# New slots for the side work between the drive matmuls of a fused tokenizer, scan and FFN kernel

## The chip, the cores and the metric

One core of a Trainium2 chip. The metric is the device time of one execution in microseconds (us), the median of several runs. "Granted clock" is the share of TensorE's full clock (2.4 GHz) that the chip let through; it has two levels here, 2.4 and 1.2 GHz.

## What is computed

For 32 images of 3x224x224 the reference cuts 196 patches of 16x16x3, normalises them, multiplies by a 768x256 matrix and normalises again (tokens). 77 text tokens of 256 values are put behind them, so that there are 273 positions. Then a gated scan and a gated FFN are added, each on a layer-normalised input:

```python
x_sub = x[:, ::2]                               # every second position
x_proj, gate = split(rmsnorm(x_sub) @ w_in.T + b_in)
h = tanh(h * A + xt[:, :, None] * Bm)           # one step per sub-sampled position
y = h @ Cm.sum(0) + Dv * xt
out = repeat((y * silu(gate)) @ w_out.T + b_out, 2)
h = h + out
h = h + (silu(n(h) @ wg.T) * (n(h) @ wu.T)) @ wd.T
```

The scan's state has 256 x 64 values for each of 32 batch rows, and its steps depend on each other.

## The kernel before, in words

The 273 positions go through the kernel in 20 groups of 14 (14 image groups, 6 text groups, the last one shorter). In the body of group i five stages run side by side on five different groups: the raw pixels of group i+1 are normalised ("ahead"), group i becomes tokens, a projection and a gate ("pre"), group i-1 is scanned ("scan"), group i-2 gets its attention output, residual and the first half of the FFN ("post"), and group i-3 the down projection ("down").

The scan sets the order of everything. A group has 7 steps of 8 chunks, 56 **slots**. A slot is one `grow` on VectorE (line 771: state times A into a PSUM bank, four banks in turn), one `drive` on TensorE (1218: adds x times B) and one `squash` on ScalarE (976: tanh). `grow(n)` waits for `squash(n-4)`, so VectorE can be four slots ahead at most. After the drive of every eighth slot (3, 11, 19, ...) TensorE also runs `read_step` (1228), which sums y. The `read_step` of slot 3 closes the group before.

All other work ("side work") is put behind the grow, drive or squash of a slot that a table names: `PLANS` (lines 65 to 113) gives for each kind of group the slot of each piece, for each engine. Kinds are "first" (group 0, no scan, slots mean order only), "second", "image" (bodies 2 to 13, of which 3 to 12 are a loop), "text" (14 to 19), "last" and "tail". GpSimd has no slots, only an order (`POOL_ORDER`, lines 116 to 139). Each engine runs its list strictly in order and waits on semaphores, so a piece whose input is late holds the slots behind it.

Pieces that matter here, with their lines:

- `shrink` (1389 to 1403), 8 pieces of 6 matmuls, the down projection; the first waits for `act_low_part` 5 on GpSimd (1158).
- `turn` (1250) and `xT_copy` (990), 8 each: transposes of pixels on TensorE and their copies on ScalarE; `embed` (1277), 12 pieces of 4 recorded matmuls.
- The **y chain**: `read_step` at slot 3, `y_copy` on ScalarE (978), four DMAs to memory (651), two back (657), `gating` on GpSimd (1116, two instructions at 1121 and 1125), and `attend(0)` and `attend(1)` on TensorE (1326, matmuls at 1335 and 1338), which wait for it.
- The **raw load**: three DMAs of 448 KB (352). The sync queue issues them only when all 7 `normalise` pieces of ScalarE (984) and of GpSimd (1136) are done with the pixels before; in its program they stand ahead of the gate load (644) and of the y chain's DMAs. `raw_patch` (776, instruction 778), 14 pieces on VectorE, wait for them.
- `residual`, `res_stats`, `res_variance`, `res_shift` (VectorE, 860 to 886), `fx_apply` and `fxT_copy` (ScalarE), `turn_fx` (TensorE), then `ffn` gate and up pieces (1361), `ffn_silu`, `ffn_product`, `act_high_part`, `act_low_part`.
- In group 0 `ffn_max`, `bias_split` and `flag_large` (VectorE, 498, 420, 539) and `count_large` make a flag that TensorE reads before its first drive (1526).

## Time and profile before

| | |
|---|---|
| median of 3 runs | 1426.93 us (1425.58 to 1428.28) |
| the profiled execution | 1428.12 us |
| its span, first to last instruction | 1426.3 us |
| TensorE matmul busy | 1224.9 us (86% of the span) |
| VectorE, ScalarE, GpSimd busy | 1085.5, 1001.3, 434.4 us |
| mean granted clock | 0.943 |
| a loop image group (ten) | 72.27 to 74.53 us |
| a text group | 51.78 us and up |

Times in the rows are microseconds from the span's start. PE is TensorE, PEld its weight loads, DVE VectorE, ACT ScalarE, POOL GpSimd, SPq the sync queue. The first 84.49 us are set-up and group 0, and 67.20 us follow the start of the last drive.

### The profile page before, as it was taken

The page shows a single profiled execution, that of the slowest core. Times are in us where ns is not written, and L with a number is a line of the kernel's source. Part 1 is how long each engine was busy: PE and PEld are TensorE (multiplying, and loading weights), DVE is VectorE, ACT ScalarE, POOL GpSimd, SP SyncE. Part 2 cuts the span into 40 slices and gives each one's busy share as a digit, 9 for nine tenths or more (in the row PEclk, how much of TensorE's full clock was granted, in tenths as well). Part 3 has the DMA queues.
Part 4 walks back from the last instruction along what each step waited for, and adds up shares of the span by engine and source line. Part 5 has one row for each costly group of instructions (what it writes and reads, how often), then busy time and mean ns, then how long its engine had stood idle before and what let it go on. Part 6 is the DMA issues. An engine that isn't in the chain of part 4 may idle for free.

```text
span 1426.3 us, 25870 instructions
## 1 busy us (share of the span) xinstructions
PE 1224.9 (86%) x7137; PEld 662.5 (46%) x7137; DVE 1085.5 (76%) x2412; ACT 1001.3 (70%) x1955; POOL 434.4 (30%) x437
## 2 busy tenths in 40 slices
...
GB/s 183 56 75 28 104 31 112 28 115 26 116 26 115 17 123 6 132 6 126 16 120 22 116 26 104 38 81 23 92 67 94 78 77 76 80 77 58 75 36 15
DMA packets 154671, 99.60 MB, mean 70 GB/s; under 512 B 129057, under 2 KB 143265, under 8 KB 153281
## 3 DMA queue, kind: packets, MB, share of 16 engines
...
## 4 chain that ended last, share of the span: by engine, by line
PE 36%; issue 22%; DMA 10%; ACT 9%; POOL 9%; DVE 8%; SPq 5%; POOLq 0%; DVEq 0%; ACTq 0%
PE Y L1228 6%; PE U L1218 6%; DMA y_scr<-y_fx 6%; PE P L1385 5%; PE P L1288 5%; PE P L1386 5%; DVE U L771 3%; PE P L1321 3%; DMA yT<-y_scr 3%; ACT h L976 3%; ACT rawn L987 2%; SPq L651 2%; DVE act L891 1%; POOL yT L1121 1%; POOL zT L1125 1%
## 5 line engine op out<-in xcount | busy, mean ns | idle before, releaser
L771 DVE TENSOR_TENSOR U<-h,a_col 128x512 f32<-128x512 f32 x1096 | 704.5, 689 | 147.7 <-ACT h L976 146.7
L976 ACT ACTIVATE h<-U 128x512 f32<-128x512 f32 x1096 | 608.1, 603 | 240.8 <-PE U L1218 239.1
L1218 PE MATMUL U<-x_diag,b_st 128*128 128x512 f16 x1096 | 370.2, 388 | 63.0 <-DVE U L771 45.1
L1228 PE MATMUL Y<-h,read_st 128*32 128x512 f32 x2192 | 271.0, 613 | 0.7 <-ACT h L976 0.7
L1218 PEld LDWEIGHTS U<-x_diag,b_st 128*128 128x128 f16 x1096 | 105.1, 100 | 220.8 <-DVE U L771 146.0
L1160 POOL TENSOR_TENSOR xT_act<-act,xT_act 128x448 f16<-128x448 f32 x114 | 117.5, 1040 | 195.1 <-ACT xT_act L1060 194.1
L1288 PE MATMUL P<-tok_w,xT_act 128*112 128x256 f32 x672 | 169.7, 391 | 2.3 <-ACT xT_act L993 2.3
L1288 PEld LDWEIGHTS P<-tok_w,xT_act 128*112 128x112 f32 x672 | 120.2, 182 | 54.0 <-issue 21.2
L1400 PE MATMUL P<-down_w,xT_act 128*112 128x256 bf16 x480 | 118.5, 282 | 6.9 <-POOL xT_act L1160 4.6
L1228 PEld LDWEIGHTS Y<-h,read_st 128*32 128x32 f32 x2192 | 58.2, 111 | 138.4 <-issue 114.9
L1401 PE MATMUL P<-down_w,xT_act 128*112 128x256 bf16 x480 | 117.4, 279 | 0.0
L891 DVE SCALAR_TENSOR_TENSOR act<-fsg,P 128x448 f32<-128x448 f32 x118 | 72.6, 615 | 52.5 <-PE P L1386 51.9
L1121 POOL TENSOR_TENSOR yT<-yT,gate_in 128x448 f32<-128x448 f32 x20 | 22.7, 1134 | 260.9 <-DMA yT<-y_scr 260.9
L993 ACT ACTIVATE xT_act<-P 128x384 f32<-128x384 f32 x112 | 83.2, 804 | 15.1 <-PE P L1273 13.2
L1385 PE MATMUL P<-fx_split,gate_w 128*128 128x448 f16 x228 | 81.7, 358 | 10.8 <-DVE fx_split L896 10.1
L1385 PE MATMUL P<-fx_split,up_w 128*128 128x448 f16 x236 | 86.4, 366 | 4.6 <-DVE act L891 4.6
L778 DVE BATCH_NORM_STATS2 raw_st<-raw 96x6 f32<-96x256 f32 x196 | 70.1, 410 | 24.8 <-DMA raw<-in_x 24.8
L1386 PE MATMUL P<-fx_split,up_w 128*128 128x448 f16 x236 | 86.3, 366 | 0.0
L1056 ACT ACTIVATE fsg<-P 128x448 f32<-128x448 f32 x114 | 62.4, 547 | 33.2 <-PE P L1386 30.4
L1386 PE MATMUL P<-fx_split,gate_w 128*128 128x448 f16 x228 | 81.8, 359 | 0.0
L1321 PE MATMUL P<-xaT,in_w 128*128 128x224 f32 x320 | 76.0, 369 | 6.0 <-ACT xf L1026 4.9
L1110 POOL TENSOR_TENSOR res_s<-res_s,half_th 112x4 f32<-112x4 f32 x20 | 20.6, 1028 | 189.8 <-DVE res_s L881 189.8
...
## 6 DMA issues: line engine op xcount, KB each, us to landing
...
```

What stands on the lines that cost most here:

```text
L771: dve.tensor_tensor(U[bank_of(slot)][:, :].rearrange("p (l b) -> p l b", b=B), h[:, (slot - CHUNKS) % RING, :].rearrange("p (l b) -> p l b ...
L891: dve.scalar_tensor_tensor(act[:, k, :], fsg[:, k % 2, :], ACT_SCALE * DEQUANT, up_bank(k, scan)[:, 0:4 * PT], ALU.mult, ALU.mult).then_in ...
L976: sc.activation(h[:, slot % RING, :], U[bank_of(slot)][:, :], ACT.Tanh, scale=1.0 / U_SCALE).then_inc(squashed, 1)
L1160: gp.tensor_tensor(act_lo[:, k, :], act[:, k, :], act_hi[:, k, :], ALU.subtract).then_inc(act_lo_done, 1)
L1218: pe.matmul(U[bank_of(slot)][:, :], b_st[:, c, :], x_diag[:, c, :, t * B:t * B + B], start=False, stop=True, skip_group_check=True).then_i ...
L1228: mm = pe.matmul(Y[c4 * 32:c4 * 32 + 32, :], read_st[:, t, half, :], h[:, (t * CHUNKS + half * RG + c4) % RING, :], start=(t == 0 and half ...
L1288: mm = pe.matmul(P[1 - k // 2][0:PT, (k % 2) * D:(k % 2) * D + D], xT[:, f, k // 2, (k % 2) * PT:(k % 2) * PT + PT], tok_w[:, f, :], start ...
L1321: mm = pe.matmul(P[1][:, k * TOK:k * TOK + TOK], in_w[:, j, e0:e0 + 128], xaT[:, j, :], start=(j == 0), stop=(j == DB - 1))
L1385: pe.matmul(bank, half, fx_hi[:, j, :], start=(j == 0), stop=False)
L1386: mm = pe.matmul(bank, half, fx_lo[:, j, :], start=False, stop=(j == DB - 1))
L1400: pe.matmul(bank, act_hi[:, f, k * PT:k * PT + PT], half, start=(f == 0), stop=False)
L1401: mm = pe.matmul(bank, act_lo[:, f, k * PT:k * PT + PT], half, start=False, stop=(f == HB - 1))
```

## The change

Only the tables `PLANS` and `POOL_ORDER` change. No instruction, wait, transfer or buffer is added or removed. For the image kind: `y_copy` goes from slot 0 to 3; `shrink` pieces 2 to 7 go ahead of where they were (five of the eight now stand ahead of slot 3's `read_step`, which had two); `turn` starts one slot later and ends at slot 16, where both `attend` pieces now stand; ScalarE's seven `normalise` pieces go from slots 47 to 55 to slots 43 to 53, and GpSimd's end ahead of `act_low_part` 4 and 5; the 14 `raw_patch` pieces go from 3 at slot 11, 8 at 15 and one each at 16, 17 and 18 to 2 at 12, 4 at 14, 1 at 15, 4 at 16 and 3 at 17. In "text" the residual's pieces are spread, in "first" the flag's pieces are mixed with others. The plans "second" and "tail" and GpSimd's other orders are changed in the same manner.

```diff
--- before.py
+++ after.py
@@ -64,76 +64,75 @@
 
 PLANS = {
     "image": dict(
-        shrink=(1, 1, 3, 3, 4, 4, 6, 7), turn=(7, 7, 8, 10, 12, 12, 12, 14), attend=(15, 16), average=(19, 21),
-        embed=(17, 19, 19, 20, 20, 21, 24, 25, 25, 27, 28, 28), turn_fx=(32, 32), ffn_gate=(34, 37, 40, 42, 45, 49),
-        ffn_up=(34, 39, 42, 43, 50, 52), turn_xa=(35,), project=(40, 40, 46, 48), finish=(6, 9), raw_patch=(11, 11,
-        11, 15, 15, 15, 15, 15, 15, 15, 15, 16, 17, 18), raw_means=(21,), raw_deviation=(23,), raw_variance=(24,),
-        res_stats=(21,), res_variance=(21,), res_shift=(25,), fx_low_part=(34, 34), tok_stats=(28, 32),
-        tok_shift=(29, 40), ln_stats=(35,), ln_shift=(35,), raw_shift=(32,), x_low_part=(43,), ffn_product=(36, 40,
-        44, 47, 51, 55), y_copy=(0,), xT_copy=(7, 7, 11, 11, 12, 12, 12, 14), fx_apply=(25, 26, 27, 28),
-        fxT_copy=(31, 31), tok_normalise=(27, 39), ln_apply=(34,), xaT_copy=(35,), x_copy=(39,), gate_silu=(47,),
-        ffn_silu=(32, 36, 39, 42, 45, 50), act_high_part=(41, 42, 43, 48, 49, 53), normalise=(47, 51, 54, 55, 55,
-        55, 55), residual=(21,)),
+        shrink=(1, 1, 1, 2, 2, 5, 6, 6), turn=(8, 8, 10, 12, 12, 13, 14, 16), attend=(16, 16), average=(19, 21),
+        embed=(17, 18, 19, 19, 21, 22, 23, 25, 27, 28, 28, 28), turn_fx=(30, 32), ffn_gate=(34, 38, 39, 41, 44, 49),
+        ffn_up=(34, 38, 42, 43, 50, 52), turn_xa=(37,), project=(40, 40, 46, 47), finish=(8, 9), raw_patch=(12, 12,
+        14, 14, 14, 14, 15, 16, 16, 16, 16, 17, 17, 17), raw_means=(19,), raw_deviation=(22,), raw_variance=(23,),
+        res_stats=(20,), res_variance=(20,), res_shift=(25,), fx_low_part=(34, 34), tok_stats=(27, 32),
+        tok_shift=(30, 37), ln_stats=(35,), ln_shift=(36,), raw_shift=(39,), x_low_part=(44,), ffn_product=(37, 40,
+        46, 47, 52, 55), y_copy=(3,), xT_copy=(7, 9, 9, 12, 12, 12, 12, 14), fx_apply=(25, 25, 27, 27),
+        fxT_copy=(30, 30), tok_normalise=(28, 37), ln_apply=(34,), xaT_copy=(36,), x_copy=(40,), gate_silu=(47,),
+        ffn_silu=(32, 37, 39, 42, 46, 50), act_high_part=(42, 42, 43, 44, 52, 53), normalise=(43, 44, 50, 50, 51,
+        53, 53), residual=(19,)),
     "text": dict(
-        shrink=(6, 7, 8, 9, 13, 16, 17, 18), attend=(23, 24), turn_fx=(34, 34), ffn_gate=(36, 39, 41, 46, 49, 50),
-        ffn_up=(37, 39, 45, 48, 49, 52), turn_xa=(26,), project=(29, 30, 31, 33), finish=(11, 21), res_stats=(31,),
-        res_variance=(31,), res_shift=(32,), fx_low_part=(36, 36), ln_stats=(23,), ln_shift=(24,), x_low_part=(45,),
-        ffn_product=(39, 45, 48, 50, 51, 55), y_copy=(3,), fx_apply=(31, 31, 31, 31), fxT_copy=(32, 32),
-        ln_apply=(23,), xaT_copy=(27,), x_copy=(30,), gate_silu=(31,), ffn_silu=(36, 39, 41, 46, 49, 50),
-        act_high_part=(45, 50, 51, 54, 55, 55), residual=(31,)),
+        shrink=(3, 5, 7, 7, 10, 15, 15, 17), attend=(21, 24), turn_fx=(34, 34), ffn_gate=(35, 38, 41, 45, 49, 52),
+        ffn_up=(36, 39, 44, 48, 50, 53), turn_xa=(27,), project=(29, 29, 32, 32), finish=(13, 20), res_stats=(32,),
+        res_variance=(32,), res_shift=(34,), fx_low_part=(36, 36), ln_stats=(22,), ln_shift=(28,), x_low_part=(46,),
+        ffn_product=(39, 43, 47, 51, 54, 55), y_copy=(2,), fx_apply=(31, 31, 31, 31), fxT_copy=(32, 32),
+        ln_apply=(26,), xaT_copy=(27,), x_copy=(29,), gate_silu=(31,), ffn_silu=(35, 38, 41, 47, 50, 53),
+        act_high_part=(43, 44, 48, 48, 53, 53), residual=(29,)),
     "last": dict(
-        shrink=(4, 7, 8, 9, 10, 13, 15, 16), attend=(23, 25), turn_fx=(33, 37), ffn_gate=(42, 45, 49, 51, 53, 55),
-        ffn_up=(42, 47, 51, 53, 55, 55), finish=(13, 19), res_stats=(37,), res_variance=(40,), res_shift=(46,),
-        fx_low_part=(48, 51), ffn_product=(52, 52, 53, 53, 53, 53), y_copy=(4,), fx_apply=(33, 38, 40, 42),
-        fxT_copy=(45, 49), ffn_silu=(53, 54, 54, 54, 55, 55), act_high_part=(54, 54, 55, 55, 55, 55),
-        residual=(30,), y_next=(50,)),
+        shrink=(2, 4, 5, 5, 7, 10, 14, 14), attend=(22, 26), turn_fx=(33, 33), ffn_gate=(35, 38, 45, 51, 51, 55),
+        ffn_up=(37, 42, 49, 53, 55, 55), finish=(15, 19), res_stats=(35,), res_variance=(40,), res_shift=(49,),
+        fx_low_part=(49, 55), ffn_product=(55, 55, 55, 55, 55, 55), y_copy=(7,), fx_apply=(35, 41, 41, 45),
+        fxT_copy=(45, 47), ffn_silu=(51, 54, 55, 55, 55, 55), act_high_part=(54, 54, 55, 55, 55, 55),
+        residual=(33,), y_next=(47,)),
     "first": dict(
-        turn=(0, 0, 0, 0, 0, 0, 0, 0), average=(27, 30), embed=(12, 13, 14, 16, 16, 16, 20, 20, 21, 22, 25, 27),
-        turn_xa=(27,), project=(30, 38, 52, 52), raw_patch=(7, 8, 11, 11, 11, 12, 12, 12, 12, 13, 13, 16, 24, 32),
-        raw_means=(35,), raw_deviation=(38,), raw_variance=(39,), tok_stats=(12, 27), tok_shift=(14, 32),
-        ln_stats=(31,), ln_shift=(34,), raw_shift=(44,), x_low_part=(48,), xT_copy=(1, 1, 2, 2, 3, 4, 6, 6),
-        tok_normalise=(21, 47), ln_apply=(22,), xaT_copy=(22,), x_copy=(30,), gate_silu=(55,), normalise=(50, 54,
-        54, 55, 55, 55, 55), count_large=(55,), flag_large=(55,), weight_copy=(2, 7, 7, 18, 20), clear_banks=(22,),
-        sum_c=(29,), read_scale=(42,), bias_split=(53,), ffn_cast=(4, 16, 25, 32, 42), ffn_max=(51, 53, 53, 53, 53,
-        53)),
+        turn=(0, 0, 0, 0, 0, 0, 0, 0), average=(13, 23), embed=(3, 4, 4, 4, 4, 4, 4, 4, 4, 4, 4, 8), turn_xa=(16,),
+        project=(19, 19, 29, 34), raw_patch=(1, 1, 1, 1, 1, 1, 1, 1, 1, 4, 9, 10, 15, 21), raw_means=(31,),
+        raw_deviation=(35,), raw_variance=(49,), tok_stats=(7, 24), tok_shift=(11, 35), ln_stats=(27,),
+        ln_shift=(27,), raw_shift=(52,), x_low_part=(51,), xT_copy=(1, 1, 1, 2, 2, 2, 4, 4), tok_normalise=(5, 33),
+        ln_apply=(20,), xaT_copy=(28,), x_copy=(34,), gate_silu=(55,), normalise=(42, 43, 43, 44, 44, 44, 44),
+        count_large=(52,), flag_large=(55,), weight_copy=(0, 3, 5, 5, 10), clear_banks=(17,), sum_c=(13,),
+        read_scale=(46,), bias_split=(45,), ffn_cast=(0, 11, 17, 39, 52), ffn_max=(38, 52, 53, 53, 54, 55)),
     "second": dict(
...
     "tail": dict(
...
 }
 
 
 POOL_ORDER = {
     "image": (
         ("gating", 0), ("res_rsqrt", 0), ("raw_rsqrt", 0), ("token_rsqrt", 0), ("token_tiles", 0), ("ln_rsqrt", 0),
-        ("normalise", 0), ("normalise", 1), ("normalise", 2), ("token_rsqrt", 1), ("token_tiles", 1),
-        ("act_low_part", 0), ("act_low_part", 1), ("normalise", 3), ("act_low_part", 2), ("act_low_part", 3),
-        ("act_low_part", 4), ("normalise", 4), ("skip_term", 0), ("act_low_part", 5), ("normalise", 5),
-        ("normalise", 6)),
+        ("token_rsqrt", 1), ("token_tiles", 1), ("normalise", 0), ("act_low_part", 0), ("normalise", 1),
+        ("act_low_part", 1), ("act_low_part", 2), ("normalise", 2), ("skip_term", 0), ("normalise", 3),
+        ("act_low_part", 3), ("normalise", 4), ("normalise", 5), ("normalise", 6), ("act_low_part", 4),
+        ("act_low_part", 5)),
     "text": (
-        ("gating", 0), ("ln_rsqrt", 0), ("res_rsqrt", 0), ("act_low_part", 0), ("skip_term", 0),
-        ("act_low_part", 1), ("act_low_part", 2), ("act_low_part", 3), ("act_low_part", 4), ("act_low_part", 5)),
+        ("gating", 0), ("ln_rsqrt", 0), ("res_rsqrt", 0), ("act_low_part", 0), ("act_low_part", 1),
+        ("skip_term", 0), ("act_low_part", 2), ("act_low_part", 3), ("act_low_part", 4), ("act_low_part", 5)),
...
```

## Rows read from the trace of the kernel before

**Rows 1.** Busy time of each engine by stretch: loop groups of 56 slots, all ten summed.

```profile
core 0: us, PE busy (x) PEld busy (x) DVE busy (x) ACT busy (x) POOL busy (x), PEclk, DMA share, GB/s
...
363.28:435.55 72.27, 63.94 (x381) 35.71 (x381) 57.59 (x135) 53.42 (x105) 24.67 (x26) 0.98 0.28 70
...
654.14:728.67 74.53, 66.52 (x381) 36.82 (x382) 57.57 (x135) 53.30 (x105) 24.65 (x26) 0.93 0.28 68
...
sum 732.43, PE 650.09 PEld 360.87 DVE 575.95 ACT 533.91 POOL 246.58; mean PE 65.01 PEld 36.09 DVE 57.60 ACT 53.39 POOL 24.66
```

**Rows 2.** Groups by shape, whole run: busy, mean ns, idle before, releaser.

```profile
L771 DVE TENSOR_TENSOR U<-h,a_col 128x512 f32<-128x512 f32 x1096 | 704.5, 689 | 147.7 <-ACT h L976 146.7
...
L1400 PE MATMUL P<-down_w,xT_act 128*112 128x256 bf16 x480 | 118.5, 282 | 6.9 <-POOL xT_act L1160 4.6 <-DVE xT_act L906 2.3
...
L778 DVE BATCH_NORM_STATS2 raw_st<-raw 96x6 f32<-96x256 f32 x196 | 70.1, 410 | 24.8 <-DMA raw<-in_x 24.8
```

**Rows 3.** Waits, whole run: total us, times, longest us.

```profile
PE P L1335 <- POOL zT L1125: 30.1, 10, 3.1
...
DVE raw_st L778 <- DMA raw<-in_x: 24.8, 12, 10.9
```

**Rows 4.** Timeline of TensorE, loop group from 363.28: attend(0).

```profile
384.14 0.54 PE L1335 MATMUL P<-bias_row,bias_one 96*112 96x512 bf16 x1 [2.92 <-POOL zT L1125]
384.47 1.91 PE L1338 MATMUL P<-out_w,zT 128*112 128x256 f32 x4
```

**Rows 5.** Timeline of the sync queue, the same group.

```profile
367.00 1.36 SPq L352 DMA_DIRECT2D raw<-in_x  x3
...
369.45 2.56 SPq L651 DMA_DIRECT2D y_scr<-y_fx  x4
378.14 1.26 SPq L657 DMA_DIRECT2D yT<-y_scr  x2
```

**Rows 6.** Timeline of ScalarE, the same group.

```profile
364.60 2.08 ACT L987 ACTIVATE rawn<-raw,raw_s 96x256 f32<-96x256 f32 x4
...
368.44 0.60 ACT L982 ACTIVATE y_fx<-Y 128x512 f32<-128x512 f32 x1 [1.28 <-PE Y L1228]
```

**Rows 7.** Busy time: slots 12 to 20 of that group, of the last image group; slots 31 to 35.

```profile
377.91:393.42 15.51, 11.88 (x66) 7.22 (x63) 11.94 (x39) 7.39 (x14) 2.27 (x2) 0.89 0.34 87
963.79:974.73 10.94, 10.06 (x63) 6.04 (x60) 7.65 (x18) 7.26 (x14) 0.27 (x2) 1.00 0.24 61
405.93:412.35 6.42, 3.98 (x22) 1.78 (x20) 6.02 (x18) 4.47 (x10) 0.29 (x1) 1.00 0.00 0
```

**Rows 8.** Timeline of the sync queue, group from 148.39.

```profile
149.72 1.26 SPq L352 DMA_DIRECT2D raw<-in_x  x3
...
153.81 1.96 SPq L651 DMA_DIRECT2D y_scr<-y_fx  x4
160.61 1.24 SPq L657 DMA_DIRECT2D yT<-y_scr  x2
```

**Rows 9.** Timeline of the sync queue, text group from 1122.07.

```profile
1127.09 1.85 SPq L651 DMA_DIRECT2D y_scr<-y_fx  x4
1130.41 1.28 SPq L657 DMA_DIRECT2D yT<-y_scr  x2
```

**Rows 10.** Busy time: last image group, and a text group.

```profile
949.15:1018.32 69.17, 63.54 (x378) 34.64 (x378) 51.45 (x102) 53.39 (x104) 20.33 (x21) 0.98 0.21 56
...
1070.29:1122.07 51.78, 48.50 (x301) 23.49 (x301) 45.36 (x85) 42.50 (x86) 11.78 (x12) 1.00 0.30 82
```

**Rows 11.** Timeline of VectorE ahead of the first drive.

```profile
65.70 2.87 DVE L501 TENSOR_REDUCE large<-act 128x1 f32<-128x1536 f32 x2
...
71.18 0.46 DVE L422 CAST bias_row<-rows 1x256 bf16<-1x256 f32 x1
...
74.86 0.15 DVE L541 TENSOR_SCALAR large_flag<-Y 1x1 int32<-1x1 f32 x1
```

**Rows 12.** Timeline of TensorE: the first drive.

```profile
84.49 0.58 PE L1218 MATMUL U<-x_diag,b_st 128*128 128x512 f16 x1 [12.99 <-issue]
```

More of the change, by code:

```diff
@@ L99 @@
-    "second": dict(
-        turn=(0, 0, 0, 0, 0, 1, 2, 2), average=(21, 22), embed=(2, 2, 6, 7, 9, 13, 23, 23, 25, 25, 28, 31),
-        turn_xa=(34,), project=(36, 39, 47, 47), raw_patch=(5, 5, 6, 6, 6, 7, 11, 14, 14, 14, 17, 17, 19, 19),
-        raw_means=(21,), raw_deviation=(22,), raw_variance=(23,), tok_stats=(25, 36), tok_shift=(26, 40),
-        ln_stats=(31,), ln_shift=(32,), raw_shift=(28,), x_low_part=(47,), xT_copy=(0, 0, 0, 0, 0, 0, 0, 1),
-        tok_normalise=(24, 39), ln_apply=(31,), xaT_copy=(35,), x_copy=(43,), gate_silu=(51,), normalise=(35, 48,
-        53, 54, 54, 55, 55), ffn_turn=(37, 40, 41, 43, 46, 49, 51, 54, 55, 55, 55), ffn_even=(37, 42, 46, 51, 53,
-        55), ffn_odd=(42, 46, 54, 55, 55)),
@@ L107 @@
-    "tail": dict(
-        shrink=(0, 0, 0, 0, 0, 5, 6, 6), attend=(2, 2), turn_fx=(7, 12), ffn_gate=(18, 43, 43, 44, 49, 53),
-        ffn_up=(42, 48, 51, 52, 54, 54), finish=(0, 2), res_stats=(0,), res_variance=(0,), res_shift=(22,),
-        fx_low_part=(29, 36), ffn_product=(41, 42, 53, 54, 55, 55), fx_apply=(0, 0, 0, 0), fxT_copy=(5, 12),
-        ffn_silu=(15, 17, 18, 22, 29, 42), act_high_part=(21, 21, 32, 53, 53, 53), residual=(0,), act_low_tail=(49,
-        54, 54, 55, 55, 55)),
+        shrink=(1, 1, 1, 2, 2, 5, 6, 6), turn=(8, 8, 10, 12, 12, 13, 14, 16), attend=(16, 16), average=(19, 21),
@@ new lines @@
+    "second": dict(
+        turn=(2, 2, 2, 2, 2, 2, 3, 3), average=(20, 21), embed=(3, 3, 5, 7, 7, 14, 23, 25, 26, 26, 29, 32),
+        turn_xa=(35,), project=(36, 37, 41, 47), raw_patch=(4, 4, 4, 4, 5, 6, 8, 13, 14, 14, 15, 15, 21, 21),
+        raw_means=(21,), raw_deviation=(22,), raw_variance=(23,), tok_stats=(23, 39), tok_shift=(26, 43),
+        ln_stats=(30,), ln_shift=(34,), raw_shift=(30,), x_low_part=(47,), xT_copy=(1, 2, 2, 2, 2, 2, 2, 3),
+        tok_normalise=(26, 40), ln_apply=(35,), xaT_copy=(35,), x_copy=(39,), gate_silu=(50,), normalise=(28, 30,
+        35, 41, 46, 47, 49), ffn_turn=(39, 39, 40, 43, 43, 46, 52, 54, 55, 55, 55), ffn_even=(39, 41, 44, 51, 54,
+        54), ffn_odd=(43, 47, 54, 55, 55)),
@@ L113 @@
+    "tail": dict(
+        shrink=(1, 1, 1, 1, 1, 5, 5, 7), attend=(1, 3), turn_fx=(28, 29), ffn_gate=(43, 45, 47, 53, 53, 53),
+        ffn_up=(45, 50, 52, 52, 54, 55), finish=(0, 5), res_stats=(0,), res_variance=(0,), res_shift=(3,),
+        fx_low_part=(12, 19), ffn_product=(41, 47, 48, 49, 52, 52), fx_apply=(0, 0, 0, 0), fxT_copy=(0, 1),
+        ffn_silu=(16, 18, 22, 30, 45, 45), act_high_part=(17, 20, 39, 40, 51, 55), residual=(0,), act_low_tail=(45,
+        47, 50, 50, 55, 55)),
 }
```

16 lines of the change are left out of this document (8 added, 8 removed).

## The prediction

> **What bounds the kernel now.** I read the busy time by stretch first. In a loop group TensorE is busy 64 to 66.5 us of 72.27 to 74.53, more than VectorE (57.6) and ScalarE (53.4); the ten take 732.43, 73.24 each [rows 1]. With the same matmuls the best such a group can reach is the 63.94 us busy of the quietest one, less what half clock added to it; the rest is waits and half clock. So I looked for the wait that holds TensorE longest. It is `attend(0)`: ten waits for `gating`, 30.1 us in all [rows 3]. In the timeline it stands idle 2.92 us, and the four matmuls behind it then run at 1.2 GHz (1.91 us) [rows 4].
>
> Why is the y chain late? The sync queue of the group, which starts at 363.28, shows it. The raw load is issued at 367.00, 3.7 us into the group; the y store at 369.45 to 372.0; the load back, which waits for the store to land, only at 378.14 [rows 5], and `attend` starts 6.0 us after that [rows 4]. From the first y store to the load back are 8.7 us. In a text group, which has no raw load, they are 3.3 us [rows 9]; in the group from 148.39, where the raw load was issued 1.3 us into the group, 6.8 us, and the load back stands at 12.2 instead of 14.9 [rows 8]. The y store lands when the 1.3 MB of pixels ahead of it have drained. The raw load itself waits for four `normalise` of ScalarE that end at 366.68, behind slot 55 [rows 6].
>
> A control stands in the same trace: the last image group has the same plan, but no raw load and no `raw_patch`. Its slots 12 to 20 take 10.94 us at granted clock 1.00, against 15.51 at 0.89 in a loop group [rows 7]. The 4.57 us are the stall, its half clock and patches on VectorE together. The whole group takes 69.17 [rows 10], 4.1 less than the mean loop group.
>
> **The change, part by part** (against the profiled execution's 1428.12 us, which is 1.19 over the median of the runs; its span is 1426.3).
>
> *Raw load and y chain, image groups.* `normalise` moves so that one squash and two `normalise` less stand behind slot 53's pieces; at 0.5 us a piece (four in 2.08, [rows 6]) ScalarE ends them 2.0 to 2.5 us earlier, and the raw load goes out at 1.2 to 1.7 into the group. GpSimd's, which now stand ahead of `act_low_part` 4 and 5, need only `raw_shift` (slot 39) and end before that; the gate's store to memory, for which the sync queue waits ahead of the raw load, needs `skip_term`, which GpSimd now runs before them too. Five shrinks instead of two stand ahead of slot 3's `read_step`; a piece of 3 and 3 matmuls takes about 0.74 us (118.5 / 480 x 3, [rows 2]), so `y_copy`, now from 368.44 (5.2 into the group, [rows 6]), ends 2.2 us later, about 8.0. By the text group's pace the load back could then go at 8.0 + 3.3 + 0.3 = 11.6, by the drained queue (12.2, 1.32 after group start, [rows 8]) at 12.2 to 12.5. The later one decides, 12.4, so `attend` may start at 18.4 instead of 20.9. The plan brings TensorE there at 17.6 + 0.22 (slot 16) + 0.4 (`turn(7)`), 18.2 at the earliest. Stall left: 0 to 0.3 us.
>
> *The patches.* Cover is what they lose. Before, 11 of 14 ran at slots 15 to 18, under the stall. Now two stand at 12, four at 14, one at 15, seven at 16 and 17: 14 x 0.41 = 5.7 us [rows 2]. From slot 12 to 16 VectorE has five grows at 0.64 us (704.5 / 1096, [rows 2]) and seven patches, 6.1 us. Against them stand some 3.1 us of TensorE (four drives, four turns and their waits for `xT_copy`, my estimate from the 10.94 us of the control) and a lead that VectorE can have, two slots, 1.3 us, so 1.7 would be bare. At 16 and 17 seven patches and two grows, 4.2 us, lie beside slot 16's turn, both attends (2.1 us: attend(0) alone took 2.3 at 1.2 GHz [rows 4], so about 1.1 each at 2.4), two drives and an embed, 4 us: nothing more is bare than what the first part leaves. I take 1.6; bounds 0 and 5.7. Net for slots 12 to 20: -4.57 + 1.6, -3.0 us a group.
>
> *Start and end of a group.* `shrink(0)` still waits for `act_low_part(5)`, which has no earlier input; the eight shrinks now fill the time in which `y_copy` no longer blocks ScalarE from slot 0. -0.2 us. ScalarE carries 1.5 us more of `normalise` before slot 53, but its lag behind the drives is what it was, since all seven stood before the next group's squashes already: 0, with +0.7 as the bound if that cover is gone.
>
> *Slots 30 to 35.* `turn_fx(0)` moves to slot 30, but needs the first two adds of `tok_stats(1)`, on VectorE at 32, as before; `raw_shift` (1.2 us) no longer stands ahead of them. -0.4 us. TensorE is busy 3.98 of 6.42 us there [rows 7]; the mean group's 73.24 is above the quiet one's 72.27 by drops that come after such stretches and the first stall. Nothing fills it in the new plan. I keep the drops: +0.8 a group over the quiet one.
>
> A loop group: 72.27 - 3.0 - 0.2 - 0.4 + 0.8 = 69.5, say 69.6: 3.6 below 73.24, -36 for ten. Bounds: 68.3 (the control without its one drop, -49) and 72.3 (-9).
>
> *Group 0.* The flag is set at 74.86, after `ffn_max` from 65.70 and `bias_split` from 71.18 [rows 11]; the first drive follows at 84.49 [rows 12]. `bias_split` (3.7 us) and `ffn_max(0)` (1.7) go into earlier idle time, but `raw_variance` now stands behind them, and with it `x_low_part` slips 1.6 us and `raw_shift` behind GpSimd's power. Net -2.2, bounds -4.3 and +2.
>
> *The other groups.* The two early scans -1. Text: residual's shift moves behind two more grows, `turn_fx` starts 0.8 us later, an earlier `x_copy` gives back 0.3: +0.5 for each of six, +3; bounds -3 and +9, since a longer wait can cost clock. The last plan puts `ffn_gate(4)` ahead of `ffn_up(3)` on one bank and `y_next` ahead of `fxT_copy(1)`: +1.5, bounds -2 and +4.
>
> Sum: -36 - 2.2 - 1 + 3 + 1.5 = -34.7. 1428.1 - 34.7 = 1393.4; less 1.2 for the median, 1392.
>
> **The price of half clock.** From 0.98 to 0.93 of granted clock a loop group goes from 72.27 to 74.53 us [rows 1]: 7 us more at 1.2 GHz cost 2.3, a third, because TensorE is not the bound in all of them. The Trainium skill (TensorE: Matmul & The Clock Gate, Terms) prices it at the throttled time times one half; by that the drops that go would bring some 6 us more than I take.
>
> **Rivals.** (1) *The clock can't be laid out.* Of two groups of the same plan one ran at 0.98 (363.28) and one at 0.93 (654.14) [rows 1], so where a drop falls is not the plan's alone. If the stall goes but as much half clock stays, 1.5 us a group are not won: +15, 1407. The Trainium skill (TensorE: Matmul & The Clock Gate, What's actually happening) has the hardware's activity monitor run free of the kernel's start, which would speak for this; no run here shows it yet. Against: the control group has no drop in slots 12 to 20.
> (2) *VectorE takes over.* The patches lie bare for 3 us rather than 1.6, ScalarE is late at slots 43 to 55 by 0.7: +2.1 a group, 1413. For: VectorE has 57.6 us of work, in lumps.
> (3) *Slower.* In slots 12 to 18 every patch lies bare, 5.7 us against the 4.57 won: +1.1 a group, +11, and with text, last group and group 0 as above, 1440. It turns when 11 of the 14 patches are bare. Against: both attends stand over seven of them.
> (4) *No effect*, the raw load goes out no earlier, because `act_high_part(5)` ahead of the last `normalise` waits for VectorE's slot 55: -9 to 0, 1424.
>
> **How the numbers follow.** Forecast (1378 to 1402) 0.55, rival 1 0.15, rival 2 0.14, rival 3 0.09, rival 4 0.07. About 2.9 us (0.2%) is what a measurement can tell from no change. Rival 4 gives half to "same". Faster 0.87, same 0.04, slower 0.09. The range runs from 1374 (control pace in all ten groups and the rest as taken: -49, so 1379, and 5 for what fewer drops could add) to 1418, past rival 2.
>
> **What would show it.** Right: PE's wait for POOL zT falls from 30.1 us to under 5; the raw load at 1.2 to 1.7 us into a group, the load back at 12 to 12.6; slots 12 to 20 in 12 to 13 us at granted clock near 1; loop groups at 69 to 70. `DVE raw_st <- DMA` nearly gone. Wrong: PE waits for DVE U at slots 13 to 18 by 3 us or more (rivals 2, 3); clock below 0.95 in loop groups (1); raw load still at 3.5 (4); text groups over 53.

## The result, and the profile after

The kernel after takes 1387.85 us (median of 4 runs, 1385.56 to 1389.87), the kernel before beside it 1427.61 (4 runs): a ratio of 0.972, interval 0.9692 to 0.9747. It is faster by 40 us, where 36 were forecast. The profiled execution took 1388.13, its span is 1386.3.

The line numbers of after are one lower than those of before. First the busy time by stretch: the loop group from 350.93, its slots 12 to 20, its slots from 32 to the `read_step` of slot 35, the last image group, a text group, and the sixth text group from 1231.16, in whose time the whole text input is loaded. They stand against [rows 1, 7, 10]. "Slots 12 to 20" means the time from the drive of slot 12 to the drive of slot 20, and so for the others.

```profile
core 0: us, PE busy (x) PEld busy (x) DVE busy (x) ACT busy (x) POOL busy (x), PEclk, DMA share, GB/s
350.93:418.27 67.34, 62.83 (x381) 34.74 (x382) 55.79 (x135) 52.93 (x105) 24.60 (x27) 1.00 0.30 75
365.42:377.92 12.50, 11.56 (x73) 7.16 (x69) 12.31 (x44) 7.91 (x14) 2.38 (x3) 1.00 0.38 100
391.17:395.89 4.72, 3.37 (x18) 1.47 (x16) 4.42 (x14) 3.60 (x8) 0.21 (x1) 1.00 0.00 0
892.31:958.11 65.80, 61.49 (x377) 34.51 (x378) 49.69 (x101) 50.84 (x101) 18.36 (x19) 1.00 0.19 52
1012.46:1066.72 54.26, 49.34 (x301) 23.20 (x302) 45.02 (x85) 42.72 (x86) 12.13 (x13) 1.00 0.29 77
1231.16:1292.23 61.07, 53.33 (x301) 24.28 (x302) 45.15 (x85) 42.80 (x86) 12.15 (x13) 0.92 0.23 57
```

Three things are to be seen. The loop group is 5 us shorter than its counterpart of 72.27, at a granted clock of 1.00; TensorE's idle time in it (span less busy) fell from 8.33 to 4.51 us. Slots 12 to 20 take 12.50 instead of 15.51. VectorE is busy in 12.31 of them, but TensorE in 11.56, and of TensorE's idle time only 0.41 us is a wait for VectorE (the row of 368.95 below). The text group got longer, 54.26 against 51.78.

The waits of the whole run, against [rows 3] (total us, times, longest):

```profile
PE P L1334 <- POOL zT L1124: 2.3, 3, 1.9
...
DVE raw_st L777 <- DMA raw<-in_x: 27.8, 3, 10.6
POOL yT L1120 <- DMA yT<-y_scr: 270.5, 19, 26.3
```

The wait of `attend(0)` fell from 30.1 us to 2.3. The patches' wait for the raw load is as large as before, but in 3 places instead of 12, none in a loop group. I had forecast it "nearly gone" and had not asked where it lies: in both kernels 20 us of it stand ahead of the first drive (9.7 and 10.6 in after), and 7.5 us now lie in the first group. GpSimd's long wait in the last row is idle time of an engine that has little to do.

Timeline of the sync queue in the group from 350.93, against [rows 5]:

```profile
352.41 1.36 SPq L351 DMA_DIRECT2D raw<-in_x  x3
354.25 0.36 SPq L643 DMA_DIRECT2D gate_in<-gate_scr  x1
359.20 1.86 SPq L650 DMA_DIRECT2D y_scr<-y_fx  x4
363.49 1.26 SPq L656 DMA_DIRECT2D yT<-y_scr  x2
```

Timeline of ScalarE in the same group, against [rows 6]: the last two `normalise` pieces, and `y_copy`:

```profile
350.96 1.13 ACT L986 ACTIVATE rawn<-raw,raw_s 96x256 f32<-96x256 f32 x2
...
358.38 0.60 ACT L981 ACTIVATE y_fx<-Y 128x512 f32<-128x512 f32 x1 [1.37 <-PE Y L1227]
```

Timeline of TensorE in the same group, around `attend` and in slots 30 to 34, against [rows 4]:

```profile
368.95 0.39 PE L1217 MATMUL U<-x_diag,b_st 128*128 128x512 f16 x1 [0.41 <-DVE U L770]
369.18 0.41 PE L1272 MATMUL P<-cst,rawn 96*128 96x96 f32 x3
369.63 0.42 PE L1334 MATMUL P<-bias_row,bias_one 96*112 96x512 bf16 x1
369.88 1.89 PE L1337 MATMUL P<-out_w,zT 128*112 128x256 f32 x8
...
390.51 0.60 PE L1356 MATMUL P<-cst,y_fx 112*128 112x112 f32 x4 [0.42 <-DVE tok L812]
390.94 0.60 PE L1217 MATMUL U<-x_diag,b_st 128*128 128x512 f16 x2
391.38 0.55 PE L1356 MATMUL P<-cst,y_fx 112*128 112x112 f32 x4
392.39 0.39 PE L1217 MATMUL U<-x_diag,b_st 128*128 128x512 f16 x1 [0.47 <-DVE U L770]
```

The raw load goes out 1.5 us into the group (before 3.7), the y store 8.3, the load back 12.6 (before 14.9), `attend` 18.7 (before 20.9), with no stall ahead of it. Its eight matmuls take 1.89 us where four took 1.91 at 1.2 GHz.

**Where 40 us come from**, by the distance between first drives (profile before less after): ten loop groups 732.43 to 676.94 us (215.37 to 892.31), about -56; the group ahead of them and the last image group -1.3 and -3.4; the first drive 7.6 us earlier (84.49 to 76.88), which the first group loses again (63.9 to 71.5 us); five text groups +12.2; the sixth, from 1231.16, +5.7 (before 55.35); the last scan and the tail +2.3. So the rest of the change gives back 20 us or so of what the image plan wins.

In the ten loop groups no half clock (time at 1.2 GHz) is left, of 65 us before. By slots, mean of the ten: 0 to 12 14.62 to 14.49; 12 to 20 15.93 to 12.50; 20 to 40 24.48 to 23.95; 40 to 56 18.21 to 16.76. Work moved over these borders too: one feed-forward piece, 0.76 us of TensorE, from behind slot 40 to ahead of it, and one `embed` and one `turn` piece, some 1.3 us, into slots 12 to 20. So only the total of 5.5 us is exact.

The start, timeline of TensorE from the flag to the first drive, against [rows 12]:

```profile
71.29 0.19 PE L536 MATMUL Y<-large 128*1 128x1 f32 x2 [6.16 <-DVE large L507]
76.88 1.44 PE L1217 MATMUL U<-x_diag,b_st 128*128 128x512 f16 x3 [5.40 <-issue]
```

The flag comes 3.3 us earlier (71.52 against 74.86 [rows 11]), and what follows it takes 5.4 us instead of 9.6. In between lies TensorE's branch into the scan's code: the trace's branch record is 4.04 us long, before 8.31.

### The profile page after: what moved, and what is told of

Same layout as the page of the kernel before. It is cut to its first block, busy times and chain, and to the rows that moved or that the text cites. A ratio compares the mean times of both kernels' runs of the same rounds, so it can differ in the third digit from the quotient of the medians.

```text
span 1386.3 us, 25870 instructions
## 1 busy us (share of the span) xinstructions
PE 1208.6 (87%) x7137; PEld 647.1 (47%) x7137; DVE 1064.6 (77%) x2412; ACT 997.0 (72%) x1955; POOL 436.1 (31%) x437
## 4 chain that ended last, share of the span: by engine, by line
PE 29%; issue 28%; POOL 17%; DVE 8%; ACT 8%; DMA 6%; SPq 2%; POOLq 1%; DVEq 0%; ACTq 0%
PE Y L1227 7%; PE U L1217 5%; DVE U L770 4%; POOL xT_act L1159 3%; POOL rawn L1140 3%; PE P L1287 3%; PE P L1399 3%; PE P L1384 3%; DMA y_scr<-y_fx 3%; PE P L1400 2%; PE P L1385 2%; ACT h L975 2%; POOL raw_s L1109 2%; DMA yT<-y_scr 2%; POOL tok L1151 2%
## 5 line engine op out<-in xcount | busy, mean ns | idle before, releaser
L770 DVE TENSOR_TENSOR U<-h,a_col 128x512 f32<-128x512 f32 x1096 | 712.6, 690 | 144.4 <-ACT h L975 140.6
L1217 PE MATMUL U<-x_diag,b_st 128*128 128x512 f16 x1096 | 374.9, 385 | 58.7 <-DVE U L770 51.6
L1227 PE MATMUL Y<-h,read_st 128*32 128x512 f32 x2192 | 267.9, 607 | 1.5 <-ACT h L975 1.5
L1384 PE MATMUL P<-fx_split,up_w 128*128 128x448 f16 x236 | 83.9, 356 | 1.0 <-DVE act L890 0.7
L1385 PE MATMUL P<-fx_split,up_w 128*128 128x448 f16 x236 | 83.6, 354 | 0.0
L1059 ACT ACTIVATE xT_act<-act 128x448 f16<-128x448 f32 x120 | 69.1, 588 | 7.3 <-DVE act L890 7.3
```

What stands on the lines that cost most here:

```text
L770: dve.tensor_tensor(U[bank_of(slot)][:, :].rearrange("p (l b) -> p l b", b=B), h[:, (slot - CHUNKS) % RING, :].rearrange("p (l b) -> p l b ...
L1217: pe.matmul(U[bank_of(slot)][:, :], b_st[:, c, :], x_diag[:, c, :, t * B:t * B + B], start=False, stop=True, skip_group_check=True).then_i ...
L1227: mm = pe.matmul(Y[c4 * 32:c4 * 32 + 32, :], read_st[:, t, half, :], h[:, (t * CHUNKS + half * RG + c4) % RING, :], start=(t == 0 and half ...
L1384: pe.matmul(bank, half, fx_hi[:, j, :], start=(j == 0), stop=False)
L1385: mm = pe.matmul(bank, half, fx_lo[:, j, :], start=False, stop=(j == DB - 1))
```

## The experiments

All are timed against the kernel before on the same chip. "Group" is the mean of the ten loop groups of the profiled run.

### The image plan alone, and all the rest alone

```diff
     "image": dict(
-        shrink=(1, 1, 3, 3, 4, 4, 6, 7), turn=(7, 7, 8, 10, 12, 12, 12, 14), attend=(15, 16), average=(19, 21),
...
+        shrink=(1, 1, 1, 2, 2, 5, 6, 6), turn=(8, 8, 10, 12, 12, 13, 14, 16), attend=(16, 16), average=(19, 21),
...
```

e1: `PLANS["image"]` and GpSimd's order for it from after, all else from before. e2: the reverse.

> The new slots for the image kind alone, all other kinds as before. Theory (the gain is the image groups', the text, last and first parts lose): ten loop groups at 67.7 us instead of 73.2 and the last image group at 65.8 instead of 69.2 give -56 and -3, so 1366 to 1372 us; text groups at 51.8, the one with the long text load at 55.4. Rival (the kinds depend on each other, so that the new text slots are part of the image groups' gain): 1380 or more, above the changed kernel's 1388 if they are needed.

> The image kind as before, all other kinds with the new slots. Theory: 1427.6 plus 5 x 2.5 for the text groups, 5.7 for the one with the long text load, 1.5 for the last scan, about 0 for the start: 1445 to 1450 us. Rival (the text groups lose because they follow the new image groups, not by their own slots): 1425 to 1432.

Measured: e1 **1369.95 us**, ratio 0.9593 (0.9568 to 0.9618), group 67.74. e2 1451.12, ratio 1.0171 (1.014 to 1.0202), group 73.3, 1 us above its theory's range. Windows of e1: the ten loop groups, one of them, a text group:

```profile
216.07:893.47 677.40, 628.37 (x3811) 347.58 (x3811) 558.31 (x1341) 529.39 (x1042) 246.02 (x261) 1.00 0.30 75
352.04:419.28 67.24, 62.84 (x382) 34.75 (x382) 55.71 (x135) 52.83 (x105) 24.61 (x27) 1.00 0.31 75
1012.85:1064.64 51.79, 48.49 (x302) 23.48 (x302) 45.37 (x85) 42.54 (x86) 11.81 (x12) 1.00 0.31 81
```

The whole gain is the image plan's, about 58 us; the other plans cost 18 (after less e1) to 23 us (e2 less before). The kernel of e1 beats both.

### What in the image plan does it: raw load, clock, `raw_shift`

e3: before with ScalarE's `normalise` at the slots of after and GpSimd's order of after. Nothing else moves.

```diff
-act_high_part=(41, 42, 43, 48, 49, 53), normalise=(47, 51, 54, 55, 55,
-        55, 55), residual=(21,)),
+act_high_part=(41, 42, 43, 48, 49, 53), normalise=(43, 44, 50, 50, 51,
+        53, 53), residual=(21,)),
```

> The kernel before, with only the seven normalise pieces of ScalarE at slots 43 to 53 and GpSimd's new order in the image kind, so that the raw load goes out early. Theory (the raw load ahead of the y store makes the attention stall): raw load at about 1.3 us into a loop group instead of 3.6, load back at 12.2 to 12.6 instead of 14.9, TensorE's wait for gating from 2.9 to under 0.7 us, slots 12 to 20 without half clock; loop groups about 70.5, total 1398 to 1405 us. Rival (the clock is what counts and falls for other waits): the stall goes but loop groups keep 3.4 us of half clock, 1410 to 1418. Rival (VectorE holds these slots): 1420 and more.

e4: before, with the wait left where it is, and 12 matmuls of constants ahead of `attend(0)` in loop groups, so that TensorE works through the stall. They go into the bank that `attend` then starts anew.

```diff
-                pe.wait_ge(z_done, q + 1)
-
                 if pre and image:
                     pe.wait_ge(xT_done, g * 8 + 7)
+                if pre and image and ahead and down and k == 0:
+                    for _ in range(12):
+                        pe.matmul(P[0][0:PT, 0:2 * D], bias_one[:, :], bias_row[:, :].unsqueeze(1).to_broadcast([BIASP, 2, D]),
+                                  start=True, stop=True, skip_group_check=True)
+                pe.wait_ge(z_done, q + 1)
+
...
```

> The kernel before with 12 more matmuls (96x512, results overwritten) in front of attend(0) in the ten loop groups, inside the time in which TensorE waits for gating anyway; the wait itself stays. Theory (the half clock after the stall costs 1.5 us of the 4.6 lost in slots 12 to 20): granted clock of these slots near 1, slots 12 to 20 in about 14.0 instead of 15.5 us, total 1409 to 1415. Rival (the half clock costs little since other engines hold the group): no more than 3 us won, 1424 to 1430.

e6: e3, and the raw input's shift on VectorE, which stood ahead of `tok_stats(1)`, back behind it.

```diff
-        tok_shift=(29, 40), ln_stats=(35,), ln_shift=(35,), raw_shift=(32,), x_low_part=(43,), ffn_product=(36, 40,
+        tok_shift=(29, 40), ln_stats=(35,), ln_shift=(35,), raw_shift=(39,), x_low_part=(43,), ffn_product=(36, 40,
```

> As e3 (raw load early, all else as before, 1408 us), but raw_shift at slot 39 instead of 32 in the image kind, so that its 1.2 us no longer stand ahead of the adds for which turn_fx waits. Theory (that wait makes the clock fall at slots 32 to 35, which the changed kernel does not show in any of ten groups): TensorE's idle time before turn_fx gone, no or few drops there, slots 32 to 36 from 9.7 on average to about 8.4, total 1393 to 1398 in all runs. Rival (the drop there comes from the waits behind turn_fx, which stay): still about 9.7 less 0.6, total 1400 to 1406 and a spread from run to run as e3.

Measured: e3 1408.51 (1392.84 to 1413.47, 5 runs), ratio 0.9865 (0.9837 to 0.9893), between its theory and its first rival. e4 1415.86, ratio 0.9917 (0.9893 to 0.9942), 1 us above its theory. e6 1385.24, ratio 0.9716 (0.9696 to 0.9735). Sync queue of e3, group from 357.18:

```profile
358.49 1.36 SPq L352 DMA_DIRECT2D raw<-in_x  x3
...
363.25 1.88 SPq L651 DMA_DIRECT2D y_scr<-y_fx  x4
369.81 1.26 SPq L657 DMA_DIRECT2D yT<-y_scr  x2
```

Here the y store goes out at 6.1 us, as early as before, and the load back still only at 12.6: it is not `y_copy` that sets this time. Moving `y_copy` to slot 3 therefore costs nothing. Windows of e3: that group, its slots 12 to 20, its slots 32 to 36; and of e4 the same three of the group from 361.06:

```profile
357.18:427.78 70.60, 63.98 (x382) 35.11 (x382) 57.25 (x135) 53.16 (x106) 24.93 (x26) 0.98 0.29 72
371.90:383.43 11.53, 10.19 (x66) 6.24 (x63) 11.38 (x38) 7.41 (x14) 2.28 (x2) 1.00 0.41 106
395.93:406.23 10.30, 7.85 (x41) 2.98 (x40) 9.12 (x24) 6.66 (x14) 1.67 (x3) 0.83 0.00 0
```

```profile
361.06:432.76 71.70, 66.46 (x393) 36.62 (x393) 57.62 (x135) 53.32 (x105) 24.71 (x26) 0.98 0.28 70
375.70:389.50 13.80, 12.99 (x78) 7.73 (x74) 12.15 (x40) 7.39 (x14) 2.27 (x2) 1.00 0.37 96
402.00:412.18 10.18, 7.74 (x41) 3.01 (x40) 9.00 (x24) 6.67 (x14) 3.30 (x6) 0.83 0.00 0
```

e4 prices the clock with the wait kept. `attend(0)` starts 20.8 us into the group, as before (20.9), so the wait is whole; slots 12 to 20 take 13.92 instead of 15.93 (mean), and 4.8 us of half clock a group are gone there: 2.0 us, 0.42 of the time at 1.2 GHz. But a drop to 1.2 GHz then came at slots 32 to 36 in nine of ten groups, in before in five. e3 takes the wait as well: 11.52 us for slots 12 to 20, the same drops at 32 in five groups of its profiled run, and about 1 us more at slots 52 to 55 (8.64 instead of 7.69 from slot 48), where ScalarE now carries `normalise` with the old places for the rest.

e6 shows what stands behind the drop at slot 32. In before and e3 `turn_fx` waits there 0.66 us a group for VectorE's adds to `tok`, which stand behind `raw_shift`; in e6 that wait is gone. Without it slots 30 to 40 take 11.19 at their quickest (before 11.87), the drops there fall from five to two of ten groups (two more come at slots 0 and 1), and 23 us of the total are won, twice the theory's 10 to 15. A part of these 23 is e3's spread from run to run: its profiled run was its fastest, 1392.84, at a mean granted clock of 0.962, its other four ran at 0.942 to 0.950. Against the profiled one e6 is 8 us faster, and its ten loop groups take 69.04 us instead of 69.98.

So of the image plan's 58 us the early raw load alone brings 19 (e3), and `raw_shift` with it 42 (e6). The other 15 are not separated by a run. Most of them lie behind slot 40, which takes 19.16 us in e6 and 16.76 in e1.

### The patches

e5: e1 with `raw_patch` at the slots of before. e10: e8 (below) with the patches begun earlier.

```diff
-raw_patch=(12, 12,
-        14, 14, 14, 14, 15, 16, 16, 16, 16, 17, 17, 17), raw_means=(19,), raw_deviation=(22,), raw_variance=(23,),
+raw_patch=(11, 11,
+        11, 15, 15, 15, 15, 15, 15, 15, 15, 16, 17, 18), raw_means=(19,), raw_deviation=(22,), raw_variance=(23,),
```

```diff
-raw_patch=(12, 12,
-        14, 14, 14, 14, 15, 16, 16, 16, 16, 17, 17, 17), raw_means=(19,), raw_deviation=(22,), raw_variance=(23,),
+raw_patch=(10, 11,
+        12, 13, 13, 14, 15, 16, 16, 16, 16, 17, 17, 17), raw_means=(19,), raw_deviation=(22,), raw_variance=(23,),
```

> As e1 (new image slots only, 1370 us), but the 14 raw_patch pieces of the image kind back at 3 at slot 11, 8 at 15, one each at 16, 17, 18. Theory (the new place leaves 1.3 to 1.6 us of them bare): slots 12 to 20 fall from 12.5 to about 11.2 us, group 66.4, total 1355 to 1360. Rival (old slots are no better here, since the raw load lands at 8 us and eight patches at slot 15 hold the grow of 16 just before both attends): 1368 to 1376.

> Image, first and POOL order of after, second, text and last of before (the version with 1361.9 us), and in the image plan VectorE's patches of the next input begin at slot 10 instead of 12 and are spread as 10, 11, 12, 13, 13, 14, 15, then four at 16 and three at 17. Theory: slots 16 to 19 take 8.96 us in the changed kernel where nine of fourteen patches stand with no drive matmuls enough beside them; spreading them brings about half a microsecond per loop group, total 1356-1358. Rival: VectorE's time from slot 10 to slot 20 is the sum of its steps wherever they stand, and patches at 10 to 13 only delay the grows that the next drive matmuls' buffers wait for: total 1361-1368.

Measured: e5 1373.85, ratio 0.9629 (0.9608 to 0.9651), group 68.11; e10 1361.02, ratio 0.9546 (0.9513 to 0.9579), group 67.55 against 67.62 for e8. Slots 12 to 20 of e5:

```profile
367.19:380.39 13.20, 11.31 (x72) 7.09 (x69) 12.49 (x44) 8.02 (x14) 2.82 (x3) 1.00 0.40 101
```

With the old places TensorE waits 1.40 us a group for VectorE in slots 12 to 20, against 0.41 in e1: the heap of eight patches at slot 15 stands ahead of the grow of 16, and both `attend` pieces stand behind the drive of 16 (slots 12 to 20 13.67 on average, three groups with a drop; slots 20 to 30 give back 0.7 of the 1.1). It is not the stall that this heap needs for cover: in e3 it stands in the same place with the stall gone, and TensorE waits for VectorE nowhere in these slots, since `attend(0)` stands behind the drive of 15. Spreading the patches further (e10) takes 0.35 us out of slots 12 to 20 and puts 0.3 into 0 to 12. In both the rival was right, or the difference too small to tell.

### The text plan

e7: e1 with the text plan and order of after, but the residual and its statistics at the slots of before. e9: the same with after's residual, and `act_high_part` 4 and 5 at slot 55. e12: e9 with the whole feed-forward part as before.

```diff
-res_stats=(32,), res_variance=(32,), res_shift=(34,), residual=(29,)
+res_stats=(31,), res_variance=(31,), res_shift=(32,), residual=(31,)
```

```diff
-act_high_part=(43, 44, 48, 48, 53, 53)
+act_high_part=(43, 44, 48, 48, 55, 55)
```

```diff
-ffn_gate=(35, 38, 41, 45, 49, 52), ffn_up=(36, 39, 44, 48, 50, 53), ffn_silu=(35, 38, 41, 47, 50, 53)
-ffn_product=(39, 43, 47, 51, 54, 55), act_high_part=(43, 44, 48, 48, 55, 55)
+ffn_gate=(36, 39, 41, 46, 49, 50), ffn_up=(37, 39, 45, 48, 49, 52), ffn_silu=(36, 39, 41, 46, 49, 50)
+ffn_product=(39, 45, 48, 50, 51, 55), act_high_part=(45, 50, 51, 54, 55, 55)
```

> As e1 with the new text slots too, but residual, res_stats, res_variance at 31 and res_shift at 32 as before. Theory (two losses in the new text slots, 2.75 us at slots 32 to 35 from the late residual, 1.4 at slots 52 to 55 from act_high_part ahead of squash 54): the first goes, text groups at 52.7 instead of 54.3, total 1376 to 1381. Rival (the residual's place is not it): text groups stay at 54.3, total 1384 to 1389.

> The image plan and the text plan of after, with the order of POOL's steps of after; the first, second and last plans of before; of the text plan only ScalarE's copies of the next h's high halves of products 4 and 5 are put back from slot 53 to slot 55. Theory: in the changed kernel these two copies stand ahead of the squash of slot 54, and TensorE waits 1.3 us for it before slot 56; put back, slots 52 to 55 of a text group fall from 3.85 to about 2.5 us, a text group from 54.3 to about 53, and the total to 1378-1382 us (an earlier run with the residual moved as well: 1385.9). Rival: the wait before slot 56 comes of the whole delay that ScalarE has gathered since slot 34, so the groups stay at 54 and the total at 1385-1388.

> As the run before with the text plan's two high-half copies back at slot 55 (1388.9 us, text groups 54.3), and in the text plan the whole feed-forward part (its gate and up matmuls, ScalarE's silu, VectorE's products, the high-half copies) is put back to the slots of before; all else in the text plan stays new. Theory: what the end of a new text group loses comes of the last silu, which stands behind the squash of slot 53 (before: behind that of slot 50), so that the last product, and the next scan's first matmuls, come late; with the feed-forward part put back the slots from 48 on fall by about 1.3 us, a text group to 52.7-53.3, and the total to 1380-1384 us. The rest of the loss, slots 32 to 35 at 8.9 instead of 6.1, stays: it comes of the residual and its statistics standing behind slot 32 and of the eight projection matmuls ahead of slot 33. Rival: ScalarE arrives late from slot 34 and the end of the group is late wherever the feed-forward stands; text groups stay at 54 or more, total 1386-1392.

Measured: e7 1385.91, ratio 0.9716 (0.9696 to 0.9736), text groups 53.9. e9 1388.89, ratio 0.9743 (0.9706 to 0.978), text groups 54.3. e12 1384.23, ratio 0.9709 (0.9683 to 0.9736), text groups 54.75. The groups given are those without half clock for e7 and e9, and for e12 those with a drop at slot 35. e9's total lies 0.9 us above its rival's range; e12's lies at the edge of its theory's, its groups where the rival had them. Windows of a text group and of its slots 48 to 56 in e9, and of a text group, its slots 32 to 36 and 48 to 56 in e12:

```profile
1014.34:1068.61 54.27, 49.29 (x301) 23.20 (x302) 44.95 (x85) 42.89 (x87) 12.13 (x12) 1.00 0.28 77
1059.38:1068.61 9.23, 7.82 (x45) 2.88 (x45) 6.69 (x12) 7.89 (x17) 3.82 (x5) 1.00 0.34 89
```

```profile
1014.69:1069.44 54.75, 50.74 (x301) 23.57 (x302) 45.00 (x85) 42.81 (x86) 11.78 (x13) 0.97 0.28 75
1041.75:1051.08 9.33, 7.36 (x36) 3.15 (x37) 6.08 (x17) 8.32 (x19) 1.01 (x1) 0.84 0.20 62
1061.13:1069.44 8.31, 7.63 (x45) 2.97 (x44) 6.73 (x12) 6.76 (x15) 4.05 (x5) 1.00 0.18 36
```

The residual's place is worth 0.4 us a group (54.3 to 53.9), the two copies nothing. The feed-forward's place is worth 0.9 at the end of the group (9.23 to 8.31), where the theory had 1.3, but in e12 four of five text groups had a drop to 1.2 GHz at slot 35 (the fifth at slot 3). These four take 22.4 us from slot 28 to 48, the fifth 20.8 (after 21.0), so the drop costs 1.6 us; in e9 one group had one, at slot 34. So the group got no shorter. Of the 4.7 us by which the total fell 3.2 lie in the sixth text group (60.7 to 57.5). Where the end of a text group waits is to be seen on VectorE in after:

```profile
1062.70 0.69 DVE L770 TENSOR_TENSOR U<-h,a_col 128x512 f32<-128x512 f32 x1
1065.41 0.62 DVE L890 SCALAR_TENSOR_TENSOR act<-fsg,P 128x448 f32<-128x448 f32 x1 [2.02 <-ACT fsg L1055]
```

The last product waits 2.02 us for the last silu, which stands behind the squash of slot 53, before behind that of slot 50. And at slot 34 TensorE waits 1.78 us for the scaled residual:

```profile
1044.01 0.60 PE L1356 MATMUL P<-cst,y_fx 112*128 112x112 f32 x4 [1.78 <-ACT y_fx L1042]
```

### The start

e8: e1 with the plan "first" of after (that of "second" stays as before). e11: the kernel before, in which the sync queue holds the raw load of group 2 until the first drive has run.

```diff
+                if isinstance(i, int) and i == 1:
+                    sp.wait_ge(driven, 1)
+                    sp.sem_inc(passed, 1)
```

> As e1 with the new slots of the first group too; the second group as before. Theory (the flag comes 3.4 us earlier, the branch after it takes 4.0 instead of 8.3 us because the raw load no longer runs beside its code's load, and the loss in the first scan of the changed kernel is the second plan's, whose raw_patch stands at slot 4 instead of 5): first drive at 77, scan 0 at 64 to 67 us, total 1362 to 1367. Rival (the raw load 4 us later holds scan 0 whatever the plan): scan 0 at 71, no gain, 1369 to 1371.

> The kernel before, in which SP holds the load of the raw input of group 2 back until the first drive matmul has been made. Theory: in before this load (72.64 us) runs beside TensorE's branch into the loop's code, which takes 8.31 us there and 4.04 us in the changed kernel, where the load comes after it; with the load held back the branch takes about 4 us, the first drive matmul comes at about 80.2 us instead of 84.5, and scan 0 gets longer, since its first patch waits for the later load; total 1423-1430. Rival: the branch's length has another cause (the number of instructions behind it, or where they lie), the first drive matmul stays at 84.5 us, and the total rises by what scan 0 loses: 1428-1435.

Measured: e8 **1361.89 us** (1360.57 to 1363.86), ratio 0.9552 (0.9531 to 0.9574); e11 1421.76 (1412.77 to 1426.07, 10 runs), ratio 0.9969 (0.9949 to 0.999). TensorE in e11, and the sync queue of e11 at the start:

```profile
71.60 0.19 PE L537 MATMUL Y<-large 128*1 128x1 f32 x2 [3.40 <-DVE large L508]
79.90 0.58 PE L1221 MATMUL U<-x_diag,b_st 128*128 128x512 f16 x1 [8.11 <-issue]
```

```profile
80.58 1.70 SPq L352 DMA_DIRECT2D raw<-in_x  x3
82.41 1.67 SPq L757 DMA_DIRECT2D x_diag<-scan_scr  x5
```

The sync queue of before in the same time:

```profile
72.64 2.31 SPq L352 DMA_DIRECT2D raw<-in_x  x3
75.08 7.82 SPq L754 DMA_DIRECT2D x_diag<-scan_scr  x16
```

The branch record of e11 is 3.40 us long, from 76.33, where before it took 8.31 from 76.02, with the raw load issued at 72.64. The hold moves more than the raw load: the 16 loads of `x_diag` behind it on the queue, which before issues beside the branch, go out behind it too, in e11 and in after. The first drive comes 4.6 us earlier, as the theory said, and the first group gives only 0.7 back; the total is 1.2 under the theory's range. In e8 the plan "first" of after brings the first drive to 77.36 without the loss that after has: its first group takes 65.1 us, that of after 71.5. What differs in it is the plan "second". One thing that this plan does is to put four patches at slot 4 (before: from slot 5), where the raw load has not landed. VectorE of after:

```profile
86.34 1.40 DVE L777 BATCH_NORM_STATS2 raw_st<-raw 96x6 f32<-96x256 f32 x4 [7.51 <-DMA raw<-in_x]
```

But this wait of 7.51 us costs nothing by slot 12: slots 0 to 12 take 20.65 us in after and 20.98 in e8. The loss lies behind it: slots 12 to 44 take 38.08 us against 30.85, 4.0 of them from slot 36 to 44, where after has five `ffn_turn` pieces (transposes of the feed-forward weights) instead of four and TensorE waits 2.4 us for the copies of `gate_w`, against 0.4 in e8. Which piece of the plan costs how much was not run.

e8 is the best version that was run, level with e10: 64 us under before and 26 under after.

## Why the prediction was right, and where it was not

The time was 1387.85 against 1392, inside the range, on the side forecast, by the mechanism named for the stall. But the total came so close by luck, since large errors of its terms cancelled. By its steps:

**Raw load and y chain: right.** Raw load 1.5 us into the group (1.2 to 1.7 forecast), `y_copy` ended at 8.05 (8.0), load back 12.6 (12.4), `attend` 18.7 (18.4), no stall (0 to 0.3). e3 shows it alone. The step that let "the later one decide" was needed: in e3 `y_copy` is 2 us earlier and the load back is not.

**Slots 12 to 20: right in size by luck, wrong on the patches.** -3.4 against the -3.0 forecast. The sum left 1.6 us of patches bare. In after TensorE waits for VectorE 0.42 us a group there, mean of the ten. Another 1.3 us are the `embed` and `turn` pieces that the plan moved in, for which there was no term: TensorE is busy 11.49 us in after and 10.19 in e3, both at a granted clock of 1.00. The last image group, which has no patches, shows the same: its slots 12 to 20 go from 10.94 to 12.12 us. What the sum had wrong is the lead of VectorE, taken at two slots from slot 12 on: in after the two patches of slot 12 run from 363.76 to 364.50, before the drive of slot 12 at 365.42, while TensorE is in the `read_step` of slot 11. Rivals 2 and 3 fall with this. Rival 1 falls with e1 and after: no half clock in twenty loop groups. It was not empty, though: in e3, e4 and e6 half clock stayed or came in at other slots.

**"I keep the drops: +0.8" failed, and "-0.4" for slots 30 to 35 was too small.** Forecast for a loop group was -3.6, measured -5.5. The drops at slots 32 to 36 cost before 12.41 - 11.87 = 0.54 us a group and went altogether; 0.17 of that was in the sum (0.97 of drops less the 0.8 kept). TensorE's idle time from slot 30 to slot 36 fell from 2.71 us (before, group from 363.28) to 1.77, 0.94 where 0.4 was taken; e6 shows 0.68 for `raw_shift` alone. Some 0.7 more went behind slot 40, for which the sum had no term and which no run separates. The other 0.4 are the second drops of slots 12 to 20, which four of the ten groups had before and which the sum kept. The ten groups hold 19 us more than the sum had.

**The price of half clock: in between.** A third was taken, from two loop groups. e4 gives 0.42 in slots 12 to 20; the drops at slot 32 cost 0.54 for 1.71 us, 0.32, where TensorE waits for VectorE anyway. The Trainium skill (TensorE: Matmul & The Clock Gate, Terms) has one half. Both of these prices are below it. A text group of before comes near it: the one from 1173.85, with one drop (granted clock 0.97), takes 53.43 us, the one ahead of it at 1.00 51.78, 1.65 us for 3.4 us at 1.2 GHz.

**Text: the term failed.** +0.5 a group and +3 in all were taken; measured +2.45 for each of five and +5.7 for the sixth, 18 us, past even the bound of +9. It was worked out from the residual's shift and the copies behind it, and for that e7 shows 0.4. What was missed is the place of the last silu on ScalarE, 0.9 (e12), and 0.7 in slots 0 to 28 (23.3 to 24.0) which every run with the new text plan has and none separates, and some 0.45 more between slots 28 and 48, whose cause stays open. The sixth group has in after 10.2 us of half clock and a 3.3 us wait that before has at 2.9 without any; e12 and e7 give 57.5 and 58.6 there. The bound was too narrow because it was built on one moved step, not on all steps of the plan.

**Group 0: inside its bounds in sum, wrong in both parts.** -2.2 forecast, the bounds -4.3 and +2; measured -7.6 to the first drive and +7.6 after it, 0. The flag itself came 3.3 us earlier; the other 4.3 us are the branch (e11), for which there was no term. The loss is the second plan's, in slots 12 to 44 of the first group, and the term of -1 for the early scans did not have it.

**Last plan and tail:** +1.5 forecast, +2.3 measured for the last scan and the tail; in e1, with the old plan, the last scan is back at 24.3 (before 25.0, after 26.5).

**The last image group** had no term, and gained 3.4 us. It has no raw load and no stall, so this gain is the rest of the plan's: 2.6 of it lie behind slot 40 (19.08 to 16.53), where TensorE's wait of 1.63 us for the load of `x_diag` is gone.

So 19 us too little gain in the loop groups, 3 in the last image group, and 15 too little loss in text nearly cancelled. The total was closer than its terms.
